# Routing tokens to experts in two parts, with the first part's expert groups between the steps of the last attention

## The reference

```python
x = x + _L0_attn_ref(_layernorm(x, axis=-1), ...)     # state-space mixer: convolution, scan over 256 tokens, 16 states
x = x + _L0_xattn_ref(_layernorm(x, axis=-1), ctx_1024, ctx_1024, ...)   # 16 heads, 64 keys
x = x + _L0_ffn_ref(_layernorm(x, axis=-1), ...)      # experts
...
gate_scores = jax.nn.softmax(jnp.einsum('btc,ce->bte', x, Wg) + bg, axis=-1)
h = jax.nn.relu(jnp.einsum('btc,ech->bteh', x, W1) + b1)
expert_out = jnp.einsum('bteh,ehc->btec', h, W2) + b2
topk_scores, topk_idx = jax.lax.top_k(gate_scores, TOP_K)
top_probs = jax.nn.softmax(topk_scores, axis=-1)
out = jnp.sum(sel * top_probs[..., None], axis=2)
```

## Time and profile before

| what | value |
|---|---|
| median of 3 runs | 1063.56 us (1059.86 to 1065.47) |
| the profiled execution | 1065.48 us |
| its span, first to last instruction | 1063.6 us |
| PE, DVE, POOL, ACT busy | 778.0, 727.8, 690.9, 483.6 us (73%, 68%, 65%, 45%) |
| mean granted clock of PE | 0.836 of 2.4 GHz |
| moved by the queues | 137.32 MB, 129 GB/s over the span |

### The profile page before, as it was taken

The page is one execution under the profiler, slowest core; times in us unless marked ns, Lnnn a source line. Parts: engine busy times, 40 slices in busy tenths (PEclk is TensorE's granted clock), DMA queues, the critical chain, the costliest instruction groups (busy, mean ns, idle before and its releaser), DMA issues. The chain is left out here.

```text
span 1063.6 us, 11949 instructions
## 1 busy us (share of the span) xinstructions
PE 778.0 (73%) x3689; PEld 482.1 (45%) x3689; DVE 727.8 (68%) x1025; ACT 483.6 (45%) x1065; POOL 690.9 (65%) x487
## 2 busy tenths in 40 slices
PE   5666586898697678769868876766767619999980
PEld 2233242453363345335335523533433418888870
DVE  3289987989977997898799799779522123333326
ACT  3557554666466464646746463542131213232320
POOL 0159987877799679779967977976723024444450
PEclk9888788996898789879878986867786659999995
DMA  2423582472284248228324822834000047777746
GB/s 66 142 104 126 148 222 82 135 191 96 90 168 145 75 127 189 91 91 177 134 80 116 189 88 82 178 121 88 12 19 21 16 152 211 205 210 213 212 119 237
DMA packets 101855, 137.32 MB, mean 129 GB/s; under 512 B 16514, under 2 KB 75276, under 8 KB 101792
## 3 DMA queue, kind: packets, MB, share of 16 engines
q1 hardware_dynamic: 97248, 128.13, 43.4%
q0 software_dynamic: 4544, 8.44, 2.6%
HBM read 105.41 MB, written 32.04 MB: 129 GB/s over the span
## 5 line engine op out<-in xcount | busy, mean ns | idle before, releaser
L1101 POOL TENSOR_TENSOR prod<-hst,BC 128x1024 f32<-128x1024 f32 x128 | 304.1, 2376 | 121.0 <-DVE hst L1239 119.8
L1239 DVE TENSOR_TENSOR_SCAN hst<-dA,Rp 128x1024 f32<-128x1024 f32 x128 | 292.7, 2287 | 11.9 <-issue 0.4
L913 ACT ACTIVATE dA<-dtm,Aneg 128x255 f32<-128x255 f32 x512 | 216.7, 497 | 144.8 <-DVE hst L1239 144.6
L506 PE MATMUL Y<-prod,ident 128*128 128x256 f32 x512 | 167.5, 460 | 62.0 <-POOL prod L1106 55.4
L506 PEld LDWEIGHTS Y<-prod,ident 128*128 128x128 f32 x512 | 109.1, 226 | 138.1 <-POOL prod L1106 90.8
L1106 POOL TENSOR_TENSOR prod<-prod 128x512 f32<-128x512 f32 x128 | 163.4, 1276 | 10.0
L1230 DVE TENSOR_TENSOR Rp<-BC,Rp 128x1024 f32<-128x1024 f32 x128 | 156.6, 1224 | 5.4 <-DMA BC<-bcd 1.6
L1180 POOL DMA_INDIRECT y2d<-prod,BC x78 | 76.7, 984 | 94.6 <-DVE prod L1529 76.8
L1133 POOL DMA_INDIRECT xsd<-xs,slots x64 | 64.2, 1004 | 66.0 <-DVE slots L1370 53.8
L506 PE MATMUL T<-Kbd,qT 64*128 64x512 f32 x128 | 67.5, 933 | 45.8 <-DVE mx L1283 44.9
L506 PE MATMUL M<-hpad,winT 128*128 128x512 f32 x160 | 77.6, 626 | 8.0 <-ACT xh L882 7.5
(11 more groups left out here) (214 smaller groups left out, 1297.7 us busy)
## 6 DMA issues: line engine op xcount, KB each, us to landing
BC<-bcd SPq DMA_DIRECT2D x64, 1024.0 KB, 5.6
BC<-in_L_ffn_W SPq DMA_DIRECT2D x78, 256.0 KB
xsd<-blank SPq DMA_DIRECT2D x17, 1032.0 KB, 16.0
BC<-xsd SPq DMA_DIRECT2D x39, 129.0 KB
soft<-in_L_ffn_b SPq DMA_DIRECT2D x39, 64.0 KB
xin<-in_x SPq DMA_DIRECT2D x8, 256.0 KB, 3.6
x2d<-x2o SPq DMA_DIRECT2D x8, 256.0 KB
E<-x2d SPq DMA_DIRECT2D x1, 2048.0 KB, 9.2
```

What stands on the lines that cost most here:

```text
L506: return pe.matmul(o, l, r_, start=start, stop=stop, **kw)
L913: m = A(dA[:, k % RING, i, 1:SEQ], dtm[:, r % 2, d, b * SEQ + 1:(b + 1) * SEQ], ACT.Exp, scale=Aneg[:, d, c * NC + i:c * NC + i + 1])
L1101: TT(prod[:, k % RING, :, :], hst[:, k % RING, :, :], BC[:, (k // 2) % BCR, 1, :, :], ALU.mult).then_inc(s_pd, 1)
L1239: v.tensor_tensor_scan(hst[:, k % RING].rearrange("p n s -> p (n s)"), dA[:, k % RING].rearrange("p n s -> p (n s)"), U.rearrange("p n s - ...
```

## The change

The tokens are routed in two parts: rounds 0 to 5 (31 groups) and rounds 6 and 7 (15 groups), 46 in all, each with its own regions, spare rows and table. Part one's table is made right after the last scan, and the last attention's steps 3 to 36 are run in pairs inside the loop over groups, on every engine. Turned and Down have one buffer each, and the gate scores and counts of rounds 6 and 7 lie in PSUM that the groups leave free. SP stores rounds 6 and 7 and loads `acc` between group loads; three of the four parts of the end run inside the loop over groups. The core of the diff:

```diff
+class Part:
+    def __init__(self, first, last, base, group):
+        self.first, self.last, self.base, self.group = first, last, base, group
+        self.region = (last - first) * TOK
+        self.most = self.region // GROUP
+        self.groups = 2 * self.region // GROUP + EXPERTS - 1
+SPLIT = 6
+PARTS = [Part(0, SPLIT, 0, 0)]
+PARTS.append(Part(SPLIT, ROUNDS, EXPERTS * PARTS[0].region + SPARE, PARTS[0].groups))
+GROUPS = PARTS[0].groups + PARTS[1].groups
+BEFORE = 3
+FINAL_AT = PARTS[1].group + 5
...
-        Down = [Y[:, :, 0:D], Rp[:, 2, :, 0:D]]
-        Turned = [t[:, 0:GROUP] for t in T]
+        Down = Rp[:, 2, :, 0:D]
+        Yf = Y[:, :, :].rearrange("p d s -> p (d s)")
+        Turned = Yf[:, 0:GROUP]
+        Gates = [M[1][:, 0:NTT * (EXPERTS + 1)], Yf[:, 0:NTT * (EXPERTS + 1)]]
+        Counts = [M[0][:, 0:(NTT + 1) * EXPERTS], Yf[:, 0:(NTT + 1) * EXPERTS]]
...
+        def lasts(slot, first, last):
+            for n in range(first, min(last, LASTS)):
                 slot(ROUNDS + n // STEPS, n % STEPS)
+        def slots_of(j):
+            return BEFORE + 2 * j, BEFORE + 2 * j + 1
# SP
-                if r == 0:
-                    blank_spare()
+                if r in (0, SPLIT):
+                    blank_spare(r)
...
+            sp.wait_ge(s_tab, 1)
+            sp.wait_ge(s_xs, 16 * 2 * NTT * SPLIT)
+            for j in range(PARTS[1].group):
+                load_group(j)
+                if j == WR + 1:
+                    store_x2(ROUNDS - 2)
+                if j == 3 * WR:
+                    store_x2(ROUNDS - 1)
+                    sp.wait_ge(s_x2, 16 * ROUNDS)
+                    sp.wait_ge(Tp.sem, Tp.at("o", ROUNDS - 1))
+                    sp.dma_start(acc.rearrange(...), x2d[...].rearrange(...)).then_inc(s_acc, 16)
+            sp.wait_ge(s_tab, 2)
+            sp.wait_ge(s_xs, 16 * 2 * NTT * ROUNDS)
+            early = SPLIT * FINAL // ROUNDS
+            for j in range(PARTS[1].group, GROUPS):
+                load_group(j)
+                if j == PARTS[1].group + WR - 1:
+                    scattered(PARTS[1].group)
+                    for i in range(early):
+                        load_results(i)
+            for i in range(early):
+                store_out(i)
+            scattered(GROUPS)
...
# PE
+                if part_of(r):
+                    pe.wait_ge(s_xg, group_of(r + 2, 4) + 3)
...
+            lasts(last, 0, BEFORE)
             pe.wait_ge(s_yd, 4 * ROUNDS)
             tile_in(0)
             tile_in(1)
+            pe.wait_ge(s_sc, ROUNDS * STEPS)
             tile_up(0)
+            pe.wait_ge(Fv.sem, Fv.at("pos", SPLIT - 1))
             for j in range(GROUPS):
+                a, b = slots_of(j)
                 if j + 2 < GROUPS:
                     tile_in(j + 2)
+                lasts(slot, a, b)
                 if j + 1 < GROUPS:
                     tile_up(j + 1)
+                lasts(slot, b, b + 1)
                 tile_down(j)
# ACT
                 tile_relu(j)
                 if j + 2 < GROUPS:
                     tile_in(j + 2)
+                lasts(slot, a, b + 1)
# POOL
+            for j in range(GROUPS):
+                a, b = slots_of(j)
+                if j:
+                    tile_back(j - 1)
+                lasts(slot, a, b + 1)
+            tile_back(GROUPS - 1)
# DVE
+            group_table(0)
+            lasts(slot, 0, BEFORE)
             for j in range(GROUPS):
+                a, b = slots_of(j)
+                tile_relu(j)
+                if j:
+                    tile_out(j - 1)
+                lasts(slot, a, b + 1)
+                if j == group_of(ROUNDS + 1, 12) + 1:
+                    group_table(1)
+                if j == PARTS[1].group + 1:
+                    weights()
+                    v.wait_ge(s_acc, 16)
+                if FINAL_AT <= j < FINAL_AT + 2 * (SPLIT * FINAL // ROUNDS):
+                    results(*divmod(j - FINAL_AT, 2))
+            tile_out(GROUPS - 1)
+            for i in range(SPLIT * FINAL // ROUNDS, FINAL):
+                for c in range(2):
+                    results(i, c)
```

More of the change, by code:

```diff
@@ new lines, in _ @@
+            sp.wait_ge(s_tab, 2)
[10 more added lines that the diff above has]
+            scattered(GROUPS)
+            for i in range(early, FINAL):
+                load_results(i)
@@ L1061, in tile_in @@
                     act.wait_ge(s_ub, j - 1)
-                A(xg[:, j % 2, :], Turned[j % 2], ACT.Copy).then_inc(s_xg, 1)
+                A(xg[:, j % 2, :], Turned, ACT.Copy).then_inc(s_xg, 1)
             def tile_relu(j):
@@ L1078, in _ @@
                     tile_in(j + 2)
+                lasts(slot, a, b + 1)
+                if j == PARTS[1].group:
+                    act.wait_ge(Fv.sem, Fv.all(ROUNDS - 1))
+                    A(wt[:, 1, :], gaps[:, :], ACT.Exp).then_inc(s_wt, 1)
         @block.gpsimd
@@ L1173, in body, with tile_back @@
                 slot(r, k)
-            rounds(body, slot)
-            for j in range(GROUPS):
+            rounds(body)
+            lasts(slot, 0, BEFORE)
+            def tile_back(j):
                 pool.wait_ge(s_ys, j + 1)
@@ L1486, in body, with group_table @@
                 slot(r, k)
-            rounds(body, slot)
-            def group_table():
-                done = [0]
+            rounds(body)
+            tabled = [0]
+            def group_table(i):
                 def then(ins):
-                    done[0] += 1
+                    tabled[0] += 1
                     ins.then_inc(s_t, 1)
-                    v.wait_ge(s_t, done[0])
-                each = [P, EXPERTS, 2 * ROUNDS]
-                wide = [P, GROUPS, EXPERTS]
-                then(v.tensor_tensor(tiles[:, :], pos[:, (ROUNDS - 1) % 2, NTT, :], first[:, :], ALU.subtract))
+                    v.wait_ge(s_t, tabled[0])
+                part = PARTS[i]
+                n = part.groups
+                each, wide = [P, EXPERTS, part.most], [P, n, EXPERTS]
+                at = slice(part.group, part.group + n)
+                ov, pa, ps_ = over[:, :, 0:part.most], past[:, 0:n, :], pasts[:, 0:n, :]
+                then(v.tensor_tensor(tiles[:, :], pos[:, (part.last - 1) % 2, NTT, :], first[:, i, :], ALU.subtract))
@@ L1502, in group_table @@
                 then(v.tensor_scalar(tiles[:, :], tiles[:, :], 1.0 / GROUP, None, ALU.mult))
-                then(v.tensor_tensor(over[:, :, :], tiles[:, :].unsqueeze(2).to_broadcast(each),
-                                     countf[:, 0:2 * ROUNDS].unsqueeze(1).to_broadcast(each), ALU.is_gt))
-                then(v.tensor_reduce(tiles[:, :], over[:, :, :], AX.X, ALU.add))
+                then(v.tensor_tensor(ov, tiles[:, :].unsqueeze(2).to_broadcast(each),
+                                     countf[:, 0:part.most].unsqueeze(1).to_broadcast(each), ALU.is_gt))
@@ L1517, in tile_relu @@
+                then(v.tensor_scalar(table[:, 1, at], expert[:, 0:n], float(EXPERTS - 1), None, ALU.min))
+                v.sem_inc(s_tab, 1)
             def tile_relu(j):
```

170 lines of the change are left out of this document (87 added, 83 removed).

## The result

The changed kernel takes 1040.71 us (median of 4 runs, 1034.52 to 1042.74) against 1064.51 us beside it: ratio 0.9753, 95% interval 0.9711 to 0.9796. The forecast was 1031.9 us in a range from 1014 to 1052. The profiled execution took 1042.74 us with a span of 1040.9; the kernel before had a span of 1063.6.

A forecast was written before the change was run, and what follows sets the result against it. Bound by latency in the attention's short chains and SP's issue in the groups. PE at step 4 at 790.0 us, plus 92.7 mixed, 130.5 plain and 18.7 tail, gave 1031.9 us; range 1014 to 1052.

The forecast's parts named there:

- The likeliest case: Whole kernel: group work fills the attention's waits, 1031.9 us, 3.0% less than before; chance 73%.
- rival 2: Groups: five megabytes on SP's queue between group loads delay rows PE needs, up to 15 us, 1047 us; chance 12%.
- Startup: Before the mixed groups: PE waits a new 12.6 us for the first groups' rows and reaches step 4 at 790.0 us.
- Mixed groups: 13 groups interleaved with attention: 48.5 us group work, 41.2 attention, 3 waits; 92.7 us, ending at 882.7 us.
- attention work at 0.86: Mixed groups: attention's 35.4 us of PE work taken at clock 0.86, so 41.2 us, 5.8 more.
- Cover for the single buffers of Turned and Down: Plain groups: losing the second PSUM buffers priced at nothing; without cover, under 1.3 us more per group.
- Plain groups: 33 groups without attention: SP is the later engine, 130.5 us in all, PE ending at 1013.2 us.
- Moved onto its queue: ... I take 0.5, 3 us: Plain groups: six loads of results on SP's queue, each taken at 0.5 us, 3 us together.
- SP's pace of 4.01 us a group: Plain groups: SP's five transfers and two table reads take 4.01 us a group, 108.3 us for 27.
- Tail: After PE's end: six of eight batches of additions come earlier, 31.3 less 12.6, so 18.7 us.
- rivals 3 and 4: 3: clock stays low in mixed groups, 1110 us, 4%; 4: group 0 waits for the attention's end, 1079 us, 4%.
- rival 1: Mixed groups: attention steps keep their old latency with group work added, 124.5 us there, 1064 us, no change; chance 7%.

The follow-up runs named there:

- experiment 6: Changed kernel with the attention's steps 3 and 4 issued ahead of group 0 instead of behind its first products; 1025.1 us (ratio 0.967).
- experiment 5: The changed kernel run again without any edit, on another chip; 1032.4 us (ratio 0.973).
- experiments 2 and 3: 2: accumulator and results all loaded behind the last group, 1037.1 us; 3: changed kernel with accumulator in eight loads, early results in six, spread between groups, 1025.1 us.
- experiment 1: Changed kernel with all loads and additions of results moved behind the last group; 1037.7 us (ratio 0.977).
- the third run: The changed kernel unedited, run a third time, on one chip with the kernel whose large loads ACT issues; 1039.6 us (ratio 0.979).
- experiment 4: Changed kernel without mixing: the attention's steps 3 to 36 all issued ahead of group 0; 1066.4 us (ratio 1.0056 to the kernel before).
- experiment 9: Changed kernel with the accumulator's and early results' large loads issued on ACT's queue; 1040.1 us, then 1038.8 us beside the changed kernel.
- experiment 10: Kernel with large loads on ACT's queue, given five attention steps ahead of group 0 and ten row buffers too; 1030.9 us (ratio 0.970).

## Why the prediction was right

The likeliest case came true together with rival 2, which was held to be an alternative: the gain came from the attention's waits, as said, and the measured 1040.7 us lies 8.8 above the forecast, 2.5% less time than before by the ratio instead of 3.0. By its terms, against the profiled span:

- *Startup*: step 4 at 790.0 us, measured 789.93. The new wait of 12.6 us was there, and experiment 6 shows that it was avoidable.
- *Mixed groups*: 92.7 us, measured 84.1 (789.93 to 874.07). The step that failed is "attention work at 0.86", 5.8 us: the granted clock was 1.00. The rule that was set beside it (the Trainium skill, TensorE: Matmul & The Clock Gate, section on the HAM clock gate: activity releases the throttle) agrees with this stage, where PE was busy 80.5 of 84 us. The waits of 3 us were there: PE waits 3.4 us from 790 to 874. The work itself is then 80.5 us, 3.4 less than the 83.9 of the sum at the full clock; in which of its pieces wasn't looked for. So 48.5 + 35.4 = 83.9 us alone would have met the measured time, by chance. Cover for the single buffers of Turned and Down held: in the plain groups PE's steps stay 3.73 us apart where rows are there.
- *Plain groups*: 130.5 us, measured 149.1. The step that failed is "Moved onto its queue: ... I take 0.5, 3 us": the accumulator's and the results' loads were counted as issues, and 5 MB of transfers at nothing. They cost 18.1 us in experiment 5, waits and half clock together. Rival 2 had the place, both of them, and priced it at up to 15. Its argument against, that the queues' share of 0.71 leaves room, looked at a mean over the stage; the loads take their time at once. The other term, SP's pace of 4.01 us a group, isn't what holds the changed kernel: outside the two stalls its outputs are 3.73 us apart, PE's own pace. It shows only when both loads are late or in pieces, in experiments 2 and 3: 131.7 and 133.4 us, near the 130.5 (the 133.5 of experiment 1 are PE's pace and the stall at the accumulator's load). The other 9.1 us of 149.1 over 140.0 go with late signals and that chip; how much each of the two takes isn't shown.
- *Tail*: 18.7 us, measured 17.7; six batches of additions were worth 12.8 us (experiment 1) for 12.6.

The errors are -8.6, +18.6 and -1.0 us, 9.0 in all: two sizes were wrong in opposite directions, and that the sum is no further off is luck. On the chip of experiment 5 they are -9.6, +9.5 and -0.9 us and cancel, and the median of 1032.4 us is within 0.5 of the forecast for that reason only; in the third run they are -7.6, +15.0 and -1.0, with 1039.6 us. In the chances, rivals 3 and 4 have 8% between them where 0.07 stands for slower, and the rest of rival 1 gets a point too much; nothing hangs on it. Rivals 1, 3 and 4 fell: attention and groups overlap (84 us where 124.5 were rival 1's), the clock was full, and the groups began at 780 us. What rival 1 says in reverse, that the gain is in filling the attention's waits, experiment 4 bears out: with everything but the mixing it is gone.

As for rival 2's mechanism, the order of a ring that the Trainium skill names (DMA: Bandwidth & Descriptors, queues, rings and completion order) isn't what costs at the results' loads: with them in another queue the wait is 8.2 us for 9.3. For the accumulator's load it is neither shown nor ruled out. The same page of the Trainium skill, in its section on issuing engines, says that transfers of all of them run on the same 16 DMA engines and interleave; experiment 9 agrees in its times, 1038.8 us against 1039.6, with no gain from the second queue.

## What to carry to other kernels

Price a moved transfer by its bytes at the time that it runs, not by its issue and not by the stage's mean share: 2 MB at once in a stage that leaves a quarter of the bandwidth cost 6 to 10 us on the chips without late signals, and in eight pieces they nearly hid. When two waits are found, remove one and read again before you add up both: behind a stall lies the pace of the next slowest engine. And where in-order engines wait on each other in turn, lay independent work between the steps: that was the whole of the gain here, and the same again at the start, where the change had left PE a new wait, gave 7.2 us more. Compare an edit's two sides in the same condition: here a profile with late signals made the early loads of results look as if they cost the plain groups 15.6 us, where it was 6.5 without.

## What was not expected

In the first profile DVE and ACT wait for signals of PE long after the products' records end. PE, then DVE's output of group 15, whose product is the first row (the part of it in the window shown) and ends at 887.3 us:

```profile
885.79 1.50 PE L571 MATMUL Rp<-BC,prod 128*128 128x128 f32 x12
887.35 1.89 PE L571 MATMUL M<-prod,BC 128*128 128x256 f32 x8
894.18 3.03 PE L571 MATMUL Rp<-BC,prod 128*128 128x128 f32 x13 [4.94 <-DVE prod L1627]
```

```profile
893.61 0.42 DVE L1627 TENSOR_TENSOR prod<-Rp,soft 128x256 f32<-128x256 f32 x1 [7.18 <-remote]
```

That is four waits of DVE and four of ACT, the longest 7.2 and 8.1 us. They are in all five profiles of the chips 3 and 13 and of the first one, at nearly the same groups (DVE's waits at 5, 13, 15 and 17 in the first, at 5, 13, 14 and 16 in three more) in kernels with different transfers, and in none of the eight profiles of the chips 2 and 10; so they go with the chip and not with an edit of the changed kernel. Each chip was used at one time only, so chip and time can't be told apart. In experiment 10, whose attention's steps come one group earlier, the late signals do too (4, 12, 13 and 15): they keep to a place in the program. The one profile of the kernel before has none in its last attention and groups; whether the change brings them on such a chip is open. The plain groups of the changed kernel are 5.5 and 9.1 us longer with them (145.5 and 149.1 against 140.0). What holds the signals isn't known; no experiment here looked for it. It is one more reason to compare kernels on one chip: the changed kernel's medians on three of them, 1032.4, 1039.6 and 1040.7 us, differ by more than several of the edits.
